# Output stage by single tiles: centred weights, ln_g and the scaled z in PSUM

## The reference, cut to what matters

```python
x = x + xattn(layernorm(x), ctx, ctx)            # gated linear attention, first stage
x = x + ffn(layernorm(x))                        # the rest, with S=512 tokens, 32 batches, E=512, 16 experts
# ffn, n batches as rows of the gather, h experts:
idx  = sort(top_k(softmax(h @ Wg)^T, 2))         # each expert takes 2 of the 32 batch rows at each position
q, k, v = hg @ Wq + bq, hg @ Wk + bk, hg @ Wv + bv
p    = softmax(q k^T * scale, axis=1)            # 2 x 2 per expert and position
ao   = (p @ v) @ Wo + bo
y    = t + zeros.at[rows].add(ao)                # scatter-add to the token rows, t = layernorm(x)
out  = x + (y - mean(y)) * rsqrt(var(y) + 1e-5) * ln_g + ln_b
```

## Time and profile before

| | us |
|---|---|
| median of 3 runs | 1842.59 (1842.56 to 1843.97) |
| profiled execution | 1843.14, span 1841.3 |
| PE busy, share of the span | 1571.0, 85% |
| DVE busy | 1414.6, 77% |
| POOL busy | 1266.8, 69% |
| ACT busy | 1210.4, 66% |
| granted TensorE clock, mean | 0.963 of full |

### The profile page before, as it was taken

The page is one execution under the profiler, slowest core; times in us unless marked ns, Lnnn a source line. Parts: engine busy times, 40 slices in busy tenths (PEclk is TensorE's granted clock), DMA queues, the critical chain, the costliest instruction groups (busy, mean ns, idle before and its releaser), DMA issues. The chain is left out here.

```text
span 1841.3 us, 58322 instructions
## 1 busy us (share of the span) xinstructions
PE 1571.0 (85%) x21933; PEld 1273.1 (69%) x22061; DVE 1414.6 (77%) x3007; ACT 1210.4 (66%) x2950; POOL 1266.8 (69%) x1235
## 2 busy tenths in 40 slices
PE   4899999999999999999999996899997877777763
PEld 3777777777777777777777775799996544444431
DVE  2578788787787787787787777687755399999998
ACT  3677777777777777777777764233332887878873
POOL 1576776777777767767777776578872568687664
PEclk9999999999999999999999998899998998989987
DMA  6123222232222322323223111745653176767776
GB/s 214 54 88 105 88 97 97 88 105 88 96 97 88 104 89 90 103 88 101 92 88 106 48 37 64 272 133 158 198 148 78 28 183 146 190 167 181 187 184 160
DMA packets 82021, 217.72 MB, mean 118 GB/s; under 512 B 13136, under 2 KB 14544, under 8 KB 72784
## 3 DMA queue, kind: packets, MB, share of 16 engines
q1 hardware_dynamic: 71504, 180.42, 33.3%
q0 software_dynamic: 10240, 33.56, 6.1%
HBM read 146.82 MB, written 67.11 MB: 116 GB/s over the span
## 5 line engine op out<-in xcount | busy, mean ns | idle before, releaser
L316 POOL TENSOR_TENSOR rec_hn<-rec_hn,rec_out_w 128x512 f32<-128x512 f32 x128 | 199.7, 1560 | 180.1 <-DVE rec_hn L743 180.1
L294 POOL TENSOR_TENSOR rec_hrs<-rec_harg,rec_minus_half 128x8 f32<-128x8 f32 x128 | 253.8, 1983 | 10.0
L1316 POOL TENSOR_TENSOR out_x_half<-out_x_half,ln_b 128x512 f32<-128x512 f32 x128 | 170.9, 1365 | 98.0 <-DVE out_z_half L1496 96.8
L1435 PE MATMUL out_z_ps<-probs_all,out_hot 128*128 128x512 f32 x256 | 150.3, 671 | 98.5 <-ACT probs_all L1362 52.4
L540 ACT ACTIVATE rec_d<-rec_l_ps 128x512 f32<-128x512 f32 x256 | 150.4, 587 | 41.0 <-PE rec_l_ps L448 40.7
L1004 PE MATMUL exp_q_ps<-exp_wqkv,exp_rows_t 128*128 128x192 f32 x1024 | 177.2, 327 | 0.0
L709 DVE TENSOR_TENSOR rec_c<-rec_s_ps,rec_d 128x512 f32<-128x512 f32 x256 | 164.5, 684 | 14.6 <-PE rec_s_ps L424 14.6
L1060 ACT ACTIVATE exp_rows_t<-exp_t_ps 128x512 f32<-128x512 f32 x128 | 69.4, 594 | 151.3 <-PE exp_t_ps L992 120.1
L955 POOL DMA_INDIRECT exp_x_rows<-x_scratch,rowid x128 | 135.5, 1059 | 45.3 <-issue 25.9
L763 DVE TENSOR_TENSOR rec_x_ring<-rec_x_ring,rec_hn 128x512 f32<-128x512 f32 x128 | 88.6, 692 | 100.3 <-POOL rec_hn L316 99.9
L1004 PEld LDWEIGHTS exp_q_ps<-exp_wqkv,exp_rows_t 128*128 128x128 f32 x1024 | 165.4, 190 | 0.4 <-ACT exp_rows_t L1060 0.3
(11 more groups left out here) (210 smaller groups left out, 4494.7 us busy)
## 6 DMA issues: line engine op xcount, KB each, us to landing
rec_x_ring<-in_x SPq DMA_DIRECT2D x128, 256.0 KB, 2.7
rec_ctx_ring<-in_ctx SPq DMA_DIRECT2D x128, 256.0 KB, 2.9
x_scratch<-rec_x_ring SPq DMA_DIRECT2D x128, 256.0 KB, 2.0
out_x_half<-x_scratch SPq DMA_DIRECT2D x128, 256.0 KB, 5.1
out<-out_x_half SPq DMA_DIRECT2D x128, 256.0 KB, 4.0
exp_wqkv<-in_wqkv SPq DMA_DIRECT2D x4, 1536.0 KB, 7.4
exp_x_rows<-x_scratch,rowid POOLq DMA_INDIRECT x128
wo<-in_wo SPq DMA_DIRECT2D x1, 2048.0 KB
```

The costliest lines, as they stand in the source:

```text
L294: nc.gpsimd.tensor_tensor(hrs[:, G % 2], harg[:, G % 2], mhalf[:], ALU.pow).then_inc(hrs_done, 1)
L316: nc.gpsimd.tensor_tensor(h, h, w8[:], ALU.mult).then_inc(hw_done, 1)
L1316: nc.gpsimd.tensor_tensor(xt[H % XR][:, q, :], xt[H % XR][:, q, :], lb[:], ALU.add).then_inc(xb_done, 1)
L1435: nc.tensor.matmul(z_ps[T % 3][:], hot[T % 4][:], ao[T % 4], start=True, stop=True).then_inc(z_full, 1)
```

## The change

The mean of z need not be subtracted any more: the rows of Wo and bo are centred over the 512 features in the expert stage (16 ACT operations, one matmul, two DVE operations, in units 40 to 55), and the mean of each x1 row, kept by the recurrence stage in `moments`, becomes a fourth table `centres`, which the add subtracts as a pointer scalar. In the output stage DVE has three passes per tile: `add`; `scale`, which multiplies by ln_g held in a PSUM bank and writes PSUM; `finish`, which reads that. All four tiles' variances come from ACT's squares, one tile at a time. DVE finishes 7 tiles behind its add. The PSUM banks are dealt out anew: one bank serves the sums and the rows, z has two, ln_g one, the scaled z two. The x1 ring has five halves (the fifth in v_all's first chunk) and load H + 5 follows the store of H. Of the first eight projection pieces DVE evicts the odd ones. POOL's variance and power stand after the second tile of the next half, its attend after the third. The order of pieces and of attends is by head group first. `mark` is not changed.

```diff
+                by_row(2, lambda c: var[:, c])
+                by_row(3, lambda c: moments[:, :, c, 0]).then_inc(tables_full, 1)
...
+            if 40 <= m < 40 + NE // 2:
+                act.wait_ge(out_in, 64)
+                act.wait_ge(wo_sum, m - 40)
+                nc.scalar.activation(unused[:], wo[:, m - 40, :], ACT.Copy, scale=-1.0 / z.E,
+                                     accum_out=wo_mean[:, m - 40:m - 39]).then_inc(wo_sum, 1)
+            if 48 <= m < 48 + NE // 2:
+                act.wait_ge(wo_sum, m - 47)
+                nc.scalar.activation(wo[:, m - 48, :], wo[:, m - 48, :], ACT.Identity, bias=wo_mean[:, m - 48:m - 47]
+                                     ).then_inc(wo_centred, 1)
+        act.wait_ge(wo_centred, NE // 2)
...
-    XR, ZR, LEAD, ON_ACT = 4, 2, 18, 3
+    XR, ZR, LEAD, BEHIND = 5, 8, 18, 7
...
-    r_ps = [psum(f"r_ps{i}") for i in range(2)]
-    z_ps = [psum(f"z_ps{r}") for r in range(3)]
...
+    r_ps = psum("r_ps")
+    z_ps = [psum(f"z_ps{r}") for r in range(2)]
+    g_ps = psum("g_ps")
+    zg_ps = [psum(f"zg_ps{r}") for r in range(2)]
...
-            if H + 3 < HALVES:
-                load(H + 3)
+            if H + XR < HALVES:
+                load(H + XR)
...
+        for T in range(TILES + 3):
+            if T < TILES:
+                pool.wait_ge(z_read, T + 1)
+                x1 = xt[T // 4 % XR][:, T % 4, :]
+                nc.gpsimd.tensor_tensor(x1, x1, lb[:], ALU.add).then_inc(xb_done, 1)
+            H, q = divmod(T, 4)
+            if q == 1 and H:
+                pool.wait_ge(square_done, 4 * H)
+                nc.gpsimd.tensor_tensor(ve[H % 2][:], var[H % 3][:], epsv[:, 4 * H - 4:4 * H], ALU.add).then_inc(ve_done, 1)
+                pool.wait_ge(ve_done, H)
+                if H > 3:
+                    pool.wait_ge(out_done, 4 * (H - 3))
+                nc.gpsimd.tensor_tensor(rs[H % 3][:], ve[H % 2][:], mhalf[:], ALU.pow).then_inc(rs_done, 1)
+            if q == 2 and T < TILES:
+                c, n = divmod(H + 3, 8)
+                if H == 0:
+                    attend(1, 2)
+                if n < 4 and c + 1 < NC:
+                    attend(c + 1, n)
...
+        for T in range(-LEAD, TILES + 1):
+            if T % 2 == 0 and T + LEAD < 2 * PIECES and (T + LEAD >= 16 or (T + LEAD) % 4 == 0):
                 put_projection((T + LEAD) // 2)
             if 0 <= T + 2 < TILES:
                 put_rows(T + 2)
+            if T > 0:
+                square(T - 1)
...
+            c, n = divmod(k, 4)
+            after(pe, r_read, 32 * (c - 1) + 4 * n + 3 if c else 0)
...
+            if u % 16 == 0 or u % 16 == KC:
+                pe.wait_ge(at_read, 4 * c + 2 + 2 * g)
+            if u < 8:
+                after(pe, first_read if u % 2 else p_read, u - u % 2)
+            else:
+                pe.wait_ge(p_read, 2 * u - 8)
...
-            pe.wait_ge(p_read, 16 * (S + 1))
-            after(pe, r_read, T - 1)
+            pe.wait_ge(p_read, 16 * S + 8)
+            pe.wait_ge(first_read, 8)
+            after(pe, r_read, T)
+            pe.wait_ge(at_read, sums_ahead(T))
...
+            after(pe, z_read, T - 1)
+            nc.tensor.matmul(z_ps[T % 2][:], hot[T % 4][:], ao[T % 4], start=True, stop=True).then_inc(z_full, 1)
 
...
+        def add(T):
+            H, q = divmod(T, 4)
+            if q == 0:
+                dve.wait_ge(x_in[H % XR], 64 * (H // XR + 1))
+            after(dve, zg_done, T - ZR + 1)
+            after(dve, square_done, T - ZR + 1)
+            dve.wait_ge(z_full, T + 1)
+            vec.scalar_tensor_tensor(zt[T % ZR][:], xt[H % XR][:, q, :], centres[:, T:T + 1], z_ps[T % 2][:],
+                                     ALU.subtract, ALU.add).then_inc(z_read, 1)
+
+        def scale(T):
+            dve.wait_ge(z_read, T + 1)
+            after(dve, out_done, T - 1)
+            vec.tensor_tensor(zg_ps[T % 2][:], zt[T % ZR][:], g_ps[:], ALU.mult).then_inc(zg_done, 1)
+
+        def finish(T):
+            H, q = divmod(T, 4)
+            x1 = xt[H % XR][:, q, :]
             dve.wait_ge(rs_done, H + 1)
...
+            dve.wait_ge(xb_done, T + 1)
+            dve.wait_ge(zg_done, T + 1)
+            vec.scalar_tensor_tensor(x1, zg_ps[T % 2][:], rs[(H + 1) % 3][:, q:q + 1], x1, ALU.mult, ALU.add
+                                     ).then_inc(out_done, 1)
...
+        dve.wait_ge(gain_set, 1)
+        for u in range(1, 8, 2):
+            put_projection(u)
+        for T in range(TILES + BEHIND):
+            if T >= BEHIND:
+                scale(T - BEHIND)
+            if T < TILES:
+                add(T)
+            if T >= BEHIND:
+                finish(T - BEHIND)
```

More of the change, by code:

```diff
@@ L1312, in _, with sums_ahead @@
             attend(1, n)
[L1313 to L1328, removed]
+        for T in range(TILES + 3):
[17 more added lines that the diff above has]
+                    attend(c + 1, n)
+    def sums_ahead(T):
+        return 4 + sum(1 for t in range(max(T - 2, 0)) if t % 32 in (0, 4, 8, 12) and t // 32 + 1 < NC)
     def projected(u):
@@ L1361, in put_rows @@
                 act.wait_ge(z_full, T - 3)
-            nc.scalar.activation(ao[T % 4], r_ps[T % 2][:], ACT.Copy, scale=sgs[:, T:T + 1]).then_inc(r_read, 1)
+            nc.scalar.activation(ao[T % 4], r_ps[:], ACT.Copy, scale=sgs[:, T:T + 1]).then_inc(r_read, 1)
         def mark(T):
@@ L1371, in mark, with square @@
             nc.scalar.activation(hot[T % 4][:], dist[:], ACT.Relu, bias=1.0, scale=-1.0).then_inc(hot_done, 1)
[L1373 to L1377, removed]
-                nc.scalar.activation(dump[:], zt[H % ZR][:, q, :], ACT.Square, bias=offs[H % 2][:, q:q + 1],
-                                     scale=-E ** -0.5, accum_out=agg[H % 2][:, q, 1:2]).then_inc(square_done, 1)
+        def square(T):
+            H, q = divmod(T, 4)
+            act.wait_ge(z_read, T + 1)
+            act.wait_ge(square_done, T)
+            if H >= 3:
+                act.wait_ge(ve_done, H - 2)
+            nc.scalar.activation(dump[:], zt[T % ZR][:], ACT.Square, scale=E ** -0.5,
+                                 accum_out=var[(H + 1) % 3][:, q:q + 1]).then_inc(square_done, 1)
         for n in range(4):
             put_sums(n)
-        for T in range(-LEAD, TILES):
-            if T > 0 and T % 4 == 0:
-                deviations(T // 4 - 1)
-            if T % 2 == 0 and T + LEAD < 2 * PIECES:
+        for T in range(-LEAD, TILES + 1):
+            if T % 2 == 0 and T + LEAD < 2 * PIECES and (T + LEAD >= 16 or (T + LEAD) % 4 == 0):
                 put_projection((T + LEAD) // 2)
@@ L1393, in _ @@
                 mark(T + 4)
-        deviations(HALVES - 1)
     @block.tensor
@@ L1433, in scatter @@
             pe.wait_ge(hot_done, T + 1)
-            after(pe, z_read, T - 2)
-            nc.tensor.matmul(z_ps[T % 3][:], hot[T % 4][:], ao[T % 4], start=True, stop=True).then_inc(z_full, 1)
+            after(pe, z_read, T - 1)
+            nc.tensor.matmul(z_ps[T % 2][:], hot[T % 4][:], ao[T % 4], start=True, stop=True).then_inc(z_full, 1)
         for n in range(4):
@@ L1514, in _ @@
-        scale(HALVES - 1)
-        finish(HALVES - 1)
+        dve.wait_ge(gain_set, 1)
[8 more added lines that the diff above has]
+                finish(T - BEHIND)
 def program(nc, x, ctx, consts, gate_w, gate_b, out_w, wg, wqkv, bqkv, wo_in, vecs, out, x1_dram):
```

136 lines of the change are left out of this document (53 added, 83 removed).

## The result

The changed kernel takes **1781.19 us** (median of 4 runs, 1777.72 to 1781.54); the kernel before took 1842.57 beside it (4 runs, 1840.30 to 1843.97). The ratio is 0.9664, 95% interval 0.9647 to 0.9681: 3.4% faster. The profiled execution took 1781.02 us (span 1779.1, mean granted clock 0.979 against 0.963), 62.1 less than the one of before. The forecast was 1794 with a range of 1775 to 1822, so the time lies in it, 13 us on the fast side.

What follows compares the result with a forecast made beforehand. ACT was to bound the output stage. From 1843.1 us: loop -50, start -2, tail -6, expert stage +1, POOL +3, DMA +2, clock +3, together -49, gave 1794 us; range 1775 to 1822 for 8 in 10.

Steps and rivals of the forecast that it cites:

- The bound: Output stage: ACT sets the pace at 2.53 us a tile, with DVE at 1.83 us a tile.
- The loop: Output stage, first rows to last: ACT's rows, one-hots, projections, squares and sums take 324 us against 374.4, so -50.
- cover of 0.9 us: Output loop: PE's work for two tiles takes 4.13 us against ACT's 5.07, leaving PE 0.9 us to spare.
- the coupling: Rival, output loop: ACT goes on waiting 0.48 us for PE before each of 55 projections, 1818 to 1820; chance 0.14.
- The reserves: Output stage: +3 for POOL's late power, +2 for the DMA and SP round, +3 for remaining clock dips.
- The DMA round: Rival, output stage: stores and loads alternating behind one queue become the bound at 11.6 us a round, 1814; chance 0.14.
- the stretched passes: Rival, output stage: DVE's passes stay stretched, 2.6 us a tile, 9 us more, 1803; chance 0.08.
- The stalls cost nothing: Rival, output stage: the 8 us for stalls fall away and sums cost 7, giving 1779; chance 0.14.
- The slower case: Rival, output loop: POOL's late power holds DVE, scatter stops on two z banks, PE drops to 1.2 GHz, 1937; chance 0.04.
- Start: Start of the output stage: ACT and DVE share the first eight projection evictions, -2 us.
- The expert stage: Expert stage: 16 more ACT operations lie in ACT's idle and cost nothing; PE's 16 more small products cost +1 us.
- Tail: After the last scatter: 16.2 us instead of 22.1, with one finish and three scale-finish pairs left, so -6.

Runs made afterwards that it cites:

- The first experiment: The changed kernel with ACT's square taking its bias from an SBUF pointer (a column of zeros) instead of a constant: 1799.95 us, ratio 0.9752.

## Why the prediction was right, and where not

**The bound: right.** ACT was named, and it is busy for 291 of the 300 us from 1450 on. The change does what it says: DVE's three passes are unstretched, and the gain needs the places in PSUM. All of the change but these gives a ratio of 1.011, ln_g alone in PSUM in the old order 1.026 or 0.995, the whole change 0.966. The old order with the scaled z in PSUM as well was not run, so how much the new order brings by itself is not shown.

**The loop: predicted -50 and 8 in reserves, measured -61.6.** ACT's timeline of the kernel after, one pair of tiles with a sum and one without:

```profile
1550.68 0.62 ACT L1405 ACTIVATE out_squares<-out_z 128x512 f32<-128x512 f32 x1
...
1551.30 0.39 ACT L1393 ACTIVATE out_distance<-tokid,colv 128x128 f32<-128x128 f32 x1
...
1551.93 1.33 ACT L1379 ACTIVATE out_ao_t<-out_p_ps,bo_t 128x512 f32<-128x512 f32 x2
...
1554.62 0.60 ACT L1369 ACTIVATE out_av_t<-out_r_ps 128x512 f32<-128x512 f32 x1 [0.20 <-PE out_r_ps L1431]
...
1556.03 0.69 ACT L1388 ACTIVATE probs_all<-out_r_ps,sigma_rows 128x512 f32<-128x512 f32 x1 [0.18 <-PE out_r_ps L1460]
...
1558.00 1.36 ACT L1379 ACTIVATE out_ao_t<-out_p_ps,bo_t 128x512 f32<-128x512 f32 x2
...
1562.88 0.72 ACT L1379 ACTIVATE out_ao_t<-out_p_ps,bo_t 128x512 f32<-128x512 f32 x1
```

A pair takes 4.88 us (1558.00 to 1562.88), not 5.07: each of its two squares takes 0.62 by starts and not the 0.72 of the earlier trace rows, because the bias pointer is gone. Over 124 squares that is 12.4 us: the mis-sized term. The first experiment gives it back, with 13.3 us in the loop and a pair of 5.07 us (1556.64 to 1561.71). The pair with a sum takes 6.07, 1.2 more, as worked out. No coupling is seen: 0.18 and 0.20 are the only waits in this stretch. But the cover of 0.9 us was wrongly reckoned. It set ACT's work against PE's own 4.13 us, while rows, scatter, projection and evictions hang on each other in a ring of 4.80. Against ACT's 4.88 that leaves 0.08: the coupling stayed away by little.

**The reserves (POOL 3, DMA 2, clock 3): not needed.** Three of the waits of the output stage:

```profile
DVE out_z L1517 <- PE out_z_ps L1468: 58.2, 80, 3.9
...
DVE out_x_half L1531 <- POOL out_rs L1345: 14.7, 5, 3.0
...
PE out_z_ps L1468 <- DVE out_z L1517: 0.5, 1, 0.5
```

The late power is there as foreseen, five times, 3.0 us at most. DVE soaks it up: PE waited for an add once, for 0.5 us. In the whole list no wait for a load stands. SP's round in its timeline:

```profile
1608.20 2.71 SPq L1304 DMA_DIRECT2D out<-out_x_half  x4
1615.18 1.70 SPq L1297 DMA_DIRECT2D out_x_half<-x_scratch  x4
1619.71 2.70 SPq L1304 DMA_DIRECT2D out<-v_all  x4
```

The loads issue in 1.70 us and not in the 3.22 of the earlier trace rows, where they stood right behind the stores. From the first store to the end of the load a round takes 8.7 us (1608.20 to 1616.88) in place of the 9.5 to 10.4 foretold, in a half of 9.8. The lower bound of 10.2 for the DMAs was also a slip: 1 MB at 245 GB/s is 4.3 us, twice plus 1 is 9.6. The granted clock is 1.00 throughout, and PE's longest wait in the loop is 1.6 us. These three at +8 and the square at +12.4 are the 20 us by which the loop was missed.

**The rivals.** The DMA round, the coupling and the stretched passes did not come here; the DMA round came late in the faster kernel with the one-hots on DVE, and the coupling with ACT relieved. "The stalls cost nothing" gave 1779, closest to 1781, but half by accident: it priced the sums at 7 and they cost 14; the square was what it lacked. The slower case, a scatter that stops on two z banks, did not come here. It came in the kernel before with a z bank taken away, with an idle of 3.5 us and the lower clock as described, but behind DVE's eight passes and not behind a late power.

**Start: right.** 2.1 us saved for 2 foretold. **The expert stage: +1 foretold.** The output stage began 2.6 us later, of which 2.1 are there already at the expert stage's first transposes; what is left for the stage itself is 0.5. Those transposes began at 1166.1, 1166.1 and 1168.7 in the three profiles with the old first stage and between 1166.3 and 1170.4 in the eleven with the changed one. So executions of an unchanged first stage differ by 2.6 us, as much as is to be explained; whether the change costs something there besides, where I had put nothing, is open.

**Tail: -6 foretold, -1 measured.** The last add and the end of DVE's timeline:

```profile
1760.89 0.76 DVE L1517 SCALAR_TENSOR_TENSOR out_z<-out_x_half,x_means,out_z_ps 128x512 f32<-128x512 f32 x1
...
1770.48 0.75 DVE L1531 SCALAR_TENSOR_TENSOR out_x_half<-out_zg_ps,out_rs,out_x_half 128x512 f32<-128x512 f32 x1
...
1771.97 0.75 DVE L1531 SCALAR_TENSOR_TENSOR out_x_half<-out_zg_ps,out_rs,out_x_half 128x512 f32<-128x512 f32 x1
```

The step that failed: I let DVE wait for the last power and then do one finish and three pairs. In fact scale and finish run seven tiles behind the add, so eight finishes stood open after the last add, 1.49 us apart (1770.48 to 1771.97): DVE's own work to 1772.7, and no wait in it. The 6.4 us of the last store were right.

**DVE's passes: 0.61 foretold, measured 0.66, 0.59 and 0.66 by starts.** The add now has a pointer operand (748 ns in place of 685 in the earlier trace rows), scale none. 1.91 us a tile in place of 1.83, still below ACT's 2.44.

Together: the square 12.4 and the reserves 8 too dear, the tail 5 and what lies ahead of the output stage 1.6 too cheap, 14 in all: 1794 less 14 is 1780, and the profiled execution took 1781.

## What to carry to other kernels

Price an operation by the form in which it will run (pointer or constant operand, source, destination), not by the nearest line of the same name: 0.1 us of a pointer, 124 times, was the largest single error here, 12.4 us, and the tail of 5 us, of the other sign, came from counting too few passes behind the last add. Two engines that stretch each other do it by their order in time as much as by their operands, so an edit of the order can change the price of a pass. And a bank that relieves one engine has a price where it is taken from. When the bound engine is relieved, look for the ring behind it before counting the gain: the one-hot moved to DVE was worth nothing until ACT's order was changed too, and then 16 us. And an engine that is at 96 of 100 in one stretch need not be full over the loop: read its waits there before saying that a delay will be paid in full.

## What the runs showed of the hardware

- A 512-wide square on ACT took 621 ns with a constant bias and 712 with a pointer.
- DVE's multiply of an SBUF by a PSUM tensor into PSUM took 685 ns, as long as the add of before from PSUM into SBUF; the passes with a pointer operand took 735 to 748 by median, wherever they read and wrote.
- The scale pass with both inputs in SBUF took 690 ns by median with POOL's ln_b pass cut to 4 columns, 1325 beside the full pass, and 1753 where its result went to SBUF too; POOL's own pass took 1271 to 1710 ns by median. The Trainium skill ("SBUF — State Buffer", Who interferes with whom) has the later of two such instructions block. The maxima agree: at 1721 to 1767 ns they are 1031 to 1089 above the minima, less than one undisturbed pass of POOL (1271).
- After 3.49 us without work PE came back at the lower of its two levels: 2.05 us for 16 products in place of 1.16. The kernel that had this in most halves was 47 us slower than before, at a mean granted clock of 0.947.
